# Another instruction order inside the eight-step pipeline of an AdaLN cross-attention kernel

## The reference

```
xq  = (1 + scale_q(cond))  * layernorm(x)   + shift_q(cond)
xkv = (1 + scale_kv(cond)) * layernorm(ctx) + shift_kv(cond)
q = xq @ Wq + bq ;  k, v = split(xkv @ Wkv + bkv)
attn = softmax(q k^T / sqrt(32)) ;  out = x + (attn v) @ Wp + bp
```

## Time and profile before

| | |
|---|---|
| median of 3 runs | 1309.93 us (1308.97 to 1312.77) |
| the profiled execution | 1311.49 us, its span from first to last instruction 1309.7 us |
| PE busy | 1165.9 us (89%) |
| DVE busy | 1050.9 us (80%) |
| ACT busy | 872.3 us (67%) |
| POOL busy | 841.6 us (64%) |
| mean granted TensorE clock | 0.981 |
| HBM traffic | 85 GB/s over the span |

### The profile page before, as it was taken

One profiled execution on the slowest core, in us unless ns is written; L12 is line 12 of the kernel. 1 busy time (PEld: TensorE's weight loads), 2 busy tenths in 40 slices (PEclk: granted clock), 3 DMA queues, 4 the chain that ended last, 5 costly groups with the idle time before them and its releaser, 6 DMA issues.

```text
span 1309.7 us, 32556 instructions
## 1 busy us (share of the span) xinstructions
PE 1165.9 (89%) x11072; PEld 693.8 (53%) x11072; DVE 1050.9 (80%) x1799; ACT 872.3 (67%) x1624; POOL 841.6 (64%) x941
## 2 busy tenths in 40 slices
PE   6897799898989998998989999898999999898997
PEld 2673455555555555554555555454555555454554
DVE  5746788888888888787888888787978888888896
ACT  2476667676776676676767677676766667676654
POOL 1544466767666776766666676766667675766744
PEclk9799899999999999999999999999999999999999
DMA  9010122222222222222222222222222222222222
GB/s 331 31 50 17 57 74 89 83 96 72 96 72 96 72 96 72 96 96 72 95 73 96 72 96 72 86 93 77 89 88 82 86 76 92 72 97 74 82 77 78
DMA packets 59871, 112.00 MB, mean 86 GB/s; under 512 B 6412, under 2 KB 6440, under 8 KB 59832
## 3 DMA queue, kind: packets, MB, share of 16 engines
q1 hardware_dynamic: 59832, 111.48, 25.0%
HBM read 77.90 MB, written 33.55 MB: 85 GB/s over the span
## 4 chain that ended last, share of the span: by engine, by line
PE 25%; issue 22%; POOL 18%; DVE 12%; ACT 10%; DMA 1%; POOLq 1%; ACTq 1%; DVEq 0%; SPq 0%
PE ps_q L1133 8%; PE ps_o L1201 7%; POOL xr L394 5%; POOL w_lo L432 4%; POOL xh L385 3%; PE ps_v L1116 3%; PE ps_t L1167 3%; DVE pr L876 3%; ACT junk L583 2%; POOL rstd L373 2%; DVE pr L896 2%; PE ps_s L1152 2%; PE ps_v L1186 2%; ACT xT_hi L510 2%; DVE mx L884 2%
## 5 line engine op out<-in xcount | busy, mean ns | idle before, releaser
L394 POOL TENSOR_TENSOR xr<-xr,bp_row 128x512 f32<-128x512 f32 x128 | 163.0, 1273 | 140.1 <-DMA xr<-in_x_dram 72.1
L603 ACT ACTIVATE pr<-pr,exp_scale 128x1024 f32<-128x1024 f32 x128 | 147.1, 1150 | 123.0 <-DVE pr L896 123.0
L558 ACT CAST pt_hi<-ps_t 128x512 f16<-128x512 f32 x256 | 138.0, 590 | 107.8 <-PE ps_t L1167 107.8
L846 DVE TENSOR_TENSOR xT_lo<-ps_v,xT_hi 128x512 f16<-128x512 f32 x120 | 83.0, 692 | 140.3 <-ACT xT_hi L510 140.3
L418 POOL TENSOR_TENSOR xr<-y,xr 128x512 f32<-128x512 f32 x128 | 162.5, 1270 | 25.5 <-POOL rstd L373 7.3
L425 POOL TENSOR_TENSOR half_den<-pr 128x512 f32<-128x512 f32 x128 | 162.9, 1272 | 22.8 <-DVE den L861 22.8
L432 POOL TENSOR_TENSOR w_lo<-w_tmp,w_hi 128x512 f16<-128x512 f32 x60 | 69.7, 1162 | 167.4 <-ACT w_hi L591 165.4
L884 DVE TENSOR_REDUCE mx<-ps_s 128x8 f32<-128x512 f32 x256 | 164.0, 683 | 12.4 <-PE ps_s L1152 12.4
L876 DVE SCALAR_TENSOR_TENSOR pr<-pr,ps_v 128x512 f32<-128x512 f32 x256 | 164.5, 684 | 4.4
L904 DVE TENSOR_TENSOR pt_lo<-ps_t,pt_hi 128x512 f16<-128x512 f32 x256 | 163.8, 682 | 0.2 <-ACT pt_hi L558 0.2
L896 DVE TENSOR_TENSOR pr<-ps_s,mx 128x512 f32<-128x512 f32 x256 | 163.8, 682 | 0.0
(11 more groups left out here) (162 smaller groups left out, 2348.9 us busy)
## 6 DMA issues: line engine op xcount, KB each, us to landing
x_in<-in_x_dram SPq DMA_DIRECT2D x128, 256.0 KB, 2.7
xr<-in_x_dram SPq DMA_DIRECT2D x128, 256.0 KB, 2.9
out_dram<-xr SPq DMA_DIRECT2D x128, 256.0 KB, 2.0
raw<-in_L_xcond_Wss_kv_dram SPq DMA_DIRECT2D x4, 512.0 KB, 5.4
cx<-in_ctx_dram SPq DMA_DIRECT2D x1, 2048.0 KB, 12.7
raw<-in_L_xcond_Wss_q_dram SPq DMA_DIRECT2D x4, 512.0 KB, 13.7
raw<-in_L_xcond_Wkv_dram SPq DMA_DIRECT2D x2, 1024.0 KB, 15.7
wq<-in_L_xcond_Wq_dram SPq DMA_DIRECT2D x1, 1024.0 KB, 17.0
```

The costliest lines, as they stand in the source:

```text
L394: pool.tensor_tensor(xr[:, s, :], xr[:, s, :], bp_row[:, :], ALU.add).then_inc(xr_ready, 1)
L558: act.copy(pt_hi[:, 4 * h:4 * h + 4, :], ps_t[:, h, :].rearrange("p (g n) -> p g n", g=4))\
L603: act.activation(pr[:, i % 2], pr[:, i % 2], ACT.Exp, scale=exp_scale[:, 0:1]).then_inc(exp_done, 1)
```

## The change

It touches only the order inside `step` on POOL, ACT and DVE, and four offsets. PE and SP are unchanged, and every instruction is still executed once per tile.

- ACT: `turned_o` before `output`; the exponential last; `key_blocks` third in step 7 (was last); `values` in step 2 between the halves of `turned_p` (was the end of step 1); `scaled_wq_hi(m)` in step m+3 between the halves of `turned_p` (was the end of step m+2); the row statistics of tile i+10 (was i+9), `sum_rows` between the halves of `turned_p`; one more tile's statistics, `row_moments(9)`, in the prologue.
- DVE: both maxima first, then `turned_o`; `weight_sums` fourth; the two halves of the shift interleaved with `turned_p`; `query` before `normalise_p`, which is last.
- POOL: `normalise` before `add_rows`; `residual` of tile i-4 (was i-2), just before `add_rows` needs it; the query weights last: `scaled_wq_lo(m)` at the end of step m+3 (was early in m+2), `scaled_wq(m)` at the end of step m+2 (was early in m+1).

```diff
             def step(b, i):                       # GpSimd
+                await_rows(b, i + 9)
                 half_sums(b, i - 1)
-                if 2 <= i <= 5:
-                    scaled_wq_lo(b + 1, i - 2)
-                if 1 <= i <= 4:
-                    scaled_wq(b + 1, i - 1)
-                await_rows(b, i + 9)
-                residual(b, i - 2)
                 moments(b, i + 9)
                 await_moments(b, i + 9)
+                residual(b, i - 4)
+                normalise(b, i + 9)
                 add_rows(b, i - 4)
-                normalise(b, i + 9)
+                if 3 <= i <= 6:
+                    scaled_wq_lo(b + 1, i - 3)
+                if 2 <= i <= 5:
+                    scaled_wq(b + 1, i - 2)
...
             def step(b, i):                       # ScalarE
+                turned_o(b, i - 3)
                 output(b, i - 4)
-                turned_o(b, i - 3)
+                if i == 7:
+                    key_blocks(b + 1)
                 turned_p(b, i - 2, 0)
+                if i == 2:
+                    values(b)
+                if 3 <= i <= 6:
+                    scaled_wq_hi(b + 1, i - 3)
+                sum_rows(b, i + 10)
                 turned_p(b, i - 2, 1)
-                sum_rows(b, i + 9)
+                if i == 4:
+                    query_bias(b + 1)
+                query(b, i + 4)
+                turned_x(b, i + 8)
+                sum_squares(b, i + 10)
                 if exists(b, i):
...
                     act.activation(pr[:, i % 2], pr[:, i % 2], ACT.Exp, scale=exp_scale[:, 0:1]).then_inc(exp_done, 1)
-                turned_x(b, i + 8)
-                if i == 4:
-                    query_bias(b + 1)
-                query(b, i + 4)
-                sum_squares(b, i + 9)
...
-                if 2 <= i <= 5:
-                    scaled_wq_hi(b + 1, i - 2)
-                if i == 1:
-                    values(b)
-                if i == 7:
-                    key_blocks(b + 1)
...
                         row_moments(8)
+                        row_moments(9)
...
             def step(b, i):                       # VectorE
-                turned_o(b, i - 3)
                 score_max(b, i, 0)
                 score_max(b, i, 1)
-                softmax_shift(b, i)
+                turned_o(b, i - 3)
+                softmax_shift(b, i, 0)
+                weight_sums(b, i - 1)
                 turned_p(b, i - 2, 0)
+                softmax_shift(b, i, 1)
                 turned_p(b, i - 2, 1)
                 turned_x(b, i + 8)
-                weight_sums(b, i - 1)
                 denominators(b, i - 1)
+                query(b, i + 4)
                 if isinstance(b, int) and b == 0 and i in (0, 1):
                     wp_low(i)
                 normalise_p(b, i - 1)
-                query(b, i + 4)
```

More of the change, by code:

```diff
@@ L886, in score_max, with softmax_shift @@
                        .then_inc(mx_done, 1)
-            def softmax_shift(b, off):
+            def softmax_shift(b, off, h):
                 if not exists(b, off):
                     return
[L892 to L898, removed]
+                if h == 0:
+                    wait(dve, p_turned, 2 * unit(b, off - 1))
+                hs = slice(HALF * h, HALF * (h + 1))
+                wait(dve, mx_done, 2 * unit(b, off) + h + 1)
+                dve.tensor_tensor(pr[:, off % 2, hs, :], ps_s[:, h, :].rearrange("p (h l) -> p h l", l=LKV),
+                                  mx[:, hs].unsqueeze(2).to_broadcast([P, HALF, LKV]), ALU.subtract)\
+                   .then_inc(sub_done, 1)
             def turned_p(b, off, h):
```

## The result

| | before | after |
|---|---|---|
| median | 1311.06 us (4 runs, 1308.97 to 1312.77) | 1186.19 us (4 runs, 1184.39 to 1189.13) |
| profiled execution, its span | 1311.49, 1309.7 us | 1187.75, 1186.0 us |
| mean granted TensorE clock | 0.981 | 0.985 |

The ratio is 0.905, with a 95% interval of 0.9024 to 0.9077: faster by 9.5%. The forecast was 1197 us with a range from 1188 to 1230.

What follows compares the result with a forecast made beforehand. TensorE's own 8.24 us a step was taken as the floor, with waits above it: 117 steps save 120.1 us, less 3.3 (boundary), 2 (prologue) and 1.5 (first steps), 113 in all. Forecast 1197 us, range 1188 to 1230.

Steps and rivals of the forecast that it cites:

- What bounds the kernel: Light steps: TensorE's own work takes 8.21 to 8.24 us a step, and what exceeds it is waiting.
- The loop: Heavy steps: w_lo, GpSimd's work to xh, turn_x, xT_hi, q_hi, w_hi, next w_lo: 9.78 us, whatever TensorE does.
- "Nothing" for the key and value copies: Key and value copies, moved to before uses that are over a full product away: priced at nothing.
- "Cost nothing" of the statistics: Row statistics ten tiles ahead: await_rows finds them made a step ago, the x load is in time; no cost.
- ScalarE and VectorE: Instruction slots in the new step, counted from S, the start of score; q_lo ends 0.8 us before the next score.
- The pitch: Length of each of 117 steps, 8.24 us instead of 9.267: 120.1 us saved.
- The loop boundary: PE's queue branches thirteen times, bounds nothing or 0.3 us, taken as 0.25 each: 3.3 us less saved.
- The first steps: Steps just after the prologue keep waits of their own: 1.5 us less saved.
- 1: Rival, chance 0.17: heavy steps stay above the floor if GpSimd's xh is slowed; time 1211 to 1224 us.
- rival 2: Rival, chance 0.13: VectorE becomes the bound, 7.65 us busy plus waits; 8.5 us a step gives 1227, 8.8 gives 1262.
- rival 3: Rival, chance 0.03: steps fall under TensorE's floor to VectorE's 7.65 us; 69 us less, 1128.
- 4: Rival, chance 0.05: VectorE's den waits for late half_sums; slower than before, 9.5 us a step gives 1337.

Runs made afterwards that it cites:

- the tenth experiment: Changed kernel with the third product of project (x high times weights low) left out of TensorE, 0.86 us a step: 1086.98 us.
- (4): Changed kernel with the query weights alone put back: w_lo and w_tmp second on GpSimd, w_hi last on ACT: 1366.19 us.
- (1): Kernel before with the query weights' new places alone (w_hi between the halves of turned_p, w_lo and w_tmp last on GpSimd): 1476.46 us.
- 2: Kernel before with the row statistics ten tiles ahead alone: 1372.09 us.
- (3): Kernel before with two parts together, the row statistics ten tiles ahead and the staggered query weights: 1247.4 us.
- (9): Changed kernel with VectorE's whole old order put back, the exponential still last on ACT: 1224.62 us.
- 5: Changed kernel with the row statistics back at nine tiles ahead, and without the tenth tile's statistics in the prologue: 1778.75 us.
- 6: Changed kernel with statistics nine tiles ahead, await_rows behind half_sums on GpSimd, and residual and add_rows back ahead of what they preceded before: 1322.13 us.
- the eleventh experiment: Changed kernel with GpSimd's half_sums done twice a step, 1.27 us more GpSimd work, den waiting for the second: 1192.96 us.
- the thirteenth: Changed kernel with the residual back at i-2 instead of i-4, in its new place on GpSimd: 1186.62 us, ratio 0.9055.

## Why the prediction was nearly right and its range wrong

**What bounds the kernel.** Right. TensorE's own 8.21 us is the floor, it is reached in all steps but the first few, and the tenth experiment shows that it is TensorE's.

**The loop.** Right, but not the whole of it. With w_hi a step later, w_lo's wait is gone from the list, and putting the weights back brings it back (4). A second wait held GpSimd, the one for the squares (1), and opening one of the two without the other makes the kernel slower (1, 2).

**"Nothing" for the key and value copies.** Right as a cost, but their old place was a reason for long steps that the prediction did not see. The first of its four steps of 9.88, the one behind the reciprocal at 655.62, is not the weights' loop. In the kernel before:

```profile
657.06 1.34 ACT L542 ACTIVATE vb<-v_all,v_mask 128x512 f16 x2 [1.50 <-PE ps_v L1186]
...
659.48 0.69 DVE L853 TENSOR_TENSOR oT_lo<-ps_v,oT_hi 128x512 f16<-128x512 f32 x1 [1.62 <-ACT oT_hi L518]
...
665.20 0.30 PE L1186 MATMUL ps_v<-pt_hi,vb 128*64 128x128 f16 x4 [0.86 <-DVE xT_lo L846]
```

This step is as long with w_lo's wait gone (3), 9.94, and 1.7 us longer than its neighbours; once in a batch that is some 25 us of what the change saves, an estimate. With the copy in step 2 no such step is left, in VectorE's old order either (9). No run moved the copy alone.

**"Cost nothing" of the statistics.** Right as a cost and too small as a reading. Costing edits one by one hid that they depend on one another: two of them, tried alone, slow the kernel (1, 2), and without this one the new order would be slower than before (5, 6). The sum came out because the whole step was laid out, not its parts: it puts every step at the floor, and so it did not need to know all that had held the steps above it.

**ScalarE and VectorE.** The slots laid out behind S were right: at 600.50 for S, the exponential starts at S+6.26 (forecast 6.6), q_lo ends at S+7.2 (7.4), half_sums starts at S-0.7 (-0.5), den at S+3.4 (3.4).

**Where the sum failed.** From 147 us to the last of the 117 steps it forecast a saving of 115.3 us (120.1 less 3.3 and 1.5); 124.7 were saved. The terms that were mis-sized:

- *The pitch.* The earlier trace rows give 8.21; the sum took 8.24, the spacing of light steps on VectorE's clock. Measured 8.206: 0.034 by 117, 4.0 us.
- *The loop boundary.* Put at 0.25 us thirteen times, 3.3 in all, with a bound of nothing. The branch is as long as before:

```profile
L246 PEldq COMPARE_BRANCH  x13: 76/207/243, 255.1 to 1043.1; - x13
```

  But from the first to the last lie twelve passes of 65.67 us, and eight steps of 8.21 are 65.68. The branch is handled while matmuls are still in flight. 3.3 us.
- *The first steps.* Put at 1.5 us less saved. xT_lo came late once, by 1.78 us; the reciprocal at 147.91 stands right behind it on VectorE, and TensorE's weigh waited 1.74 for it. The next reciprocal came after 7.43 us, for VectorE, without a wait, works faster than TensorE and catches up. All 117 steps are 0.6 us less than 117 of 8.206. With the 1.5, 2.1 us.

These are the 9.4 us. The prologue was put at 2 us; the second reciprocal came 0.96 later. But the first reciprocal is at 132.92 in the eleventh experiment, 134.83 in the thirteenth and 136.49 here, with the same prologue, so less than 4 us can't be read there as the price of a tile's statistics. The tail took 78.5 us both times, as forecast.

These terms are the step that failed; the mechanism of the sum, all steps at TensorE's floor, held. The low end of 1188 took the prologue, the boundary and the tail at their best, and neither the pitch nor the first steps. The changed kernel's own runs spread over 4.7 us. An end of the range that adds up only some of the small terms' bounds was too near.

**The rivals.** 1: xh keeps its duration in all 128 instructions:

```profile
L385 POOL TENSOR_SCALAR xh<-x_in,neg_mean,rstd x128: 759/768/779, 65.3 to 1095.8; 128x512 f32<-128x512 f32 x128
```

Its price, too, was too high: GpSimd past its slack costs 9 us over the 117 steps (11), not 14 to 27. 2: VectorE's true need is at most 7.39 a step, since instructions of 0.68 us follow one another 0.60 apart; with the 0.3 us of extra wait that rival 2 counted on it would still be under 8.21. 3: the floor held; with less work on TensorE the steps went under rival 3's 7.65. By the Trainium skill, Perfetto Trace Analysis, section Identifying the Most-Contended Engine, weight-load busy time, beside the share of peak arithmetic, tells how near TensorE is to its limit. It fills 40.33 of 66.00 us here, while the tenth experiment shows TensorE to be at its limit, so in this kernel the weight loads by themselves mislead. 4: real, one edit away (4, 5).

## What to carry to other kernels

Where every engine keeps its own hand-written order, lay out one whole step with a slot for each instruction: reorderings that open one loop close another unless its partner moves with it, so they can't be priced, or tried, one by one. Look first at waits that stand ahead of work which doesn't need them, and read for each kind of long step by itself what holds it: here the weights, the squares, the values and q_lo each held some. When the steps are bound by one engine, take the pitch from its own timeline rather than from another engine's clock, cost nothing that its queue does while work is in flight, and let the range hold the bounds of all the small terms together.

## What the runs showed of the hardware

- Two VectorE instructions of 128x512 that run 0.68 us each start 0.60 apart when none waits. Busy time summed from looser stretches overstates what the engine needs (7.65 against at most 7.39 a step).
- In the kernel before two xh were slow, not one as the prediction has it: 1.83 and 1.82 us, each beside one of the two wp_lo. After there is none, but a tiny instruction has taken its place:

```profile
131.56 1.42 DVE L937 SCALAR_TENSOR_TENSOR wp_lo<-xr,scale,wp_hi 128x1024 f16<-128x1024 f32 x1 [1.44 <-ACT wp_hi L624]
...
131.99 1.05 POOL L370 TENSOR_SCALAR veps<-row_sq 128x1 f32<-128x1 f32 x1
```

  veps takes 0.19 us at the median and 1.05 here and beside the second wp_lo; both times it ends 0.05 us after wp_lo. The Trainium skill (GPSIMD Engine Reference, Specifications) has this contention, for VectorE instructions with two SBUF inputs, and the trace agrees. That GpSimd is held until the VectorE instruction ends is only read from these ends; no experiment tested it.
- The granted clock follows TensorE's pauses. In 104 of the fifth experiment's 117 steps it is below 1.00, in all but two of these 0.87 on average, so partly at 1.2 and mostly at 2.4 GHz, and TensorE is busy for 9.8 us with work that takes 8.28 in the steps at 1.00. With TensorE never idle it is 1.00 in every step. In the sixth experiment it is 1.00 in all 117 too, with steps of up to 10.8 us, though TensorE is idle for some 2 us in each of the longer ones, so those pauses cost no clock there. In the kernel before it falls in 10 of 117 steps, to between 0.85 and 0.98, all of them steps of 9.78 us or more; one of 9.78 us had 0.90 and another of the same length 1.00.
